# One-hot of an edge group: four 128x128 compares with a per-partition scalar in place of one 128x512 compare of two tensors

## What is computed

```python
h = jnp.einsum('ni,hio->hno', x, W)
e = attn_src[:, src_idx] + attn_dst[:, dst_idx]
e = jnp.where(e >= 0, e, NEG_SLOPE * e)
e = e * edge_weight[None, :]
e_exp = jnp.exp(e - jnp.max(e))
denom = jax.ops.segment_sum(e_exp.T, dst_idx, num_segments=num_nodes).T
alpha = e_exp / (denom[:, dst_idx] + 1e-10)
msg = h[:, src_idx] * alpha[..., None]
out = jax.vmap(lambda m: jax.ops.segment_sum(m, dst_idx, num_segments=num_nodes))(msg)
```

## Time and profile before

| | |
|---|---|
| runs, us | 868.2, 868.28, 870.37 (median 868.28) |
| span of the profiled execution, us | 864.6 |
| mean granted TensorE clock | 0.836 |
| busy: PE, DVE, POOL, ACT, us | 709.8, 596.9, 513.7, 231.3 |
| first and last start of a gather on POOL, us | 92.8, 641.7 |
| gathers (line 380), one-hots (line 992) | 392, 98 |

### The profile page before, as it was taken

One profiled execution on the slowest core, in us unless ns is written; L12 is line 12 of the kernel. 1 busy time (PEld: TensorE's weight loads), 2 busy tenths in 40 slices (PEclk: granted clock), 3 DMA queues, 4 the chain that ended last, 5 costly groups with the idle time before them and its releaser, 6 DMA issues.

```text
span 864.6 us, 18704 instructions
## 1 busy us (share of the span) xinstructions
PE 709.8 (82%) x4369; PEld 541.9 (63%) x4370; DVE 596.9 (69%) x1630; ACT 231.3 (27%) x915; POOL 513.7 (59%) x512
## 2 busy tenths in 40 slices
PE   3799687887878798868787878787876998999995
PEld 2576665555555565545565546465555987999994
DVE  7665277565657576657675757676667991999985
ACT  1133502111212122213132323232333442333331
POOL 5242537777777777778777777777751070333332
PEclk9899799776769776777787868787787998999998
DMA  6254325554556555554555545555420002000000
GB/s 202 69 170 80 95 59 132 128 123 121 123 125 129 125 124 129 121 124 119 122 128 128 128 115 126 126 119 120 115 79 1 1 1 78 19 31 26 32 25 21
DMA packets 104859, 82.97 MB, mean 96 GB/s; under 512 B 67133, under 2 KB 91566, under 8 KB 104561
## 3 DMA queue, kind: packets, MB, share of 16 engines
q0 software_dynamic: 18816, 52.21, 22.6%
q1 hardware_dynamic: 85873, 29.16, 15.6%
HBM read 74.47 MB, written 6.84 MB: 94 GB/s over the span
## 4 chain that ended last, share of the span: by engine, by line
POOL 37%; issue 26%; PE 21%; DVE 9%; DMA 4%; SPq 2%; POOLq 1%; DVEq 0%; ACT 0%; ACTq 0%
POOL G L380 37%; PE ps L561 8%; PE ps L574 7%; PE ps L414 2%; PE ps L420 2%; DVE wprod L1086 1%; DMA x<-in_x 1%; DVE G L1069 1%; DVE x L1073 1%; DVE stats L739 1%; DVE x L1027 1%; DMA dstm_d<-wide 1%; DMA htab<-hst 1%; DVE acc L1079 1%; DMA G<-htab,srcr 1%
## 5 line engine op out<-in xcount | busy, mean ns | idle before, releaser
L380 POOL DMA_INDIRECT G<-htab,srcr x392 | 419.3, 1070 | 149.9 <-issue 138.3
L480 PE MATMUL ps<-msg,oh 128*128 128x260 f32 x784 | 303.0, 525 | 74.0 <-DVE oh L992 73.7
L480 PEld LDWEIGHTS ps<-msg,oh 128*128 128x128 f32 x784 | 176.6, 249 | 105.0 <-issue 78.9
L930 DVE TENSOR_TENSOR msg<-G,msg 128x1024 f32<-128x1024 f32 x98 | 119.8, 1222 | 32.8 <-issue 22.2
L561 PEld LDWEIGHTS ps<-xnT,w 128*128 128x128 f32 x800 | 98.3, 201 | 3.8 <-issue 1.8
L561 PE MATMUL ps<-xnT,w 128*128 128x128 f32 x800 | 98.8, 285 | 2.1 <-ACT wide L721 1.6
L663 ACT ACTIVATE negR<-ps 128x1 f32<-128x1 f32 x98 | 16.8, 171 | 291.2 <-PE ps L476 253.9
L574 PE MATMUL ps<-w,wide 128*128 128x256 f32 x400 | 90.4, 379 | 1.0 <-DVE acc L1093 1.0
L393 POOL TENSOR_SCALAR G<-acc,mw 128x256 f32<-128x256 f32 x25 | 23.1, 926 | 99.6 <-DVE mw L1126 90.4
L449 PE MATMUL ps<-ad,ohT 128*128 x1464 | 74.7, 176 | 8.7 <-issue 4.5
L992 DVE TENSOR_TENSOR oh<-iota,dmr 128x512 f32<-128x512 f32 x98 | 67.4, 687 | 19.8 <-issue 19.0
(11 more groups left out here) (137 smaller groups left out, 801.8 us busy)
## 6 DMA issues: line engine op xcount, KB each, us to landing
dstb<-dstu_d SPq DMA_DIRECT2D x98, 128.0 KB
G<-htab,srcr POOLq DMA_INDIRECT x392
htab<-hst SPq DMA_DIRECT2D x25, 130.0 KB, 3.2
out<-G SPq DMA_DIRECT2D x24, 128.0 KB, 1.7
x<-in_x SPq DMA_DIRECT2D x4, 640.0 KB, 8.0
w<-in_L_ffn_w SPq DMA_DIRECT2D x4, 512.0 KB
kq<-w_d SPq DMA_DIRECT2D x1, 1600.0 KB, 6.3
dmr<-dstm_d SPq DMA_DIRECT2D x98, 2.0 KB
```

Source lines behind the costliest of these rows:

```text
L380: gp.indirect_dma_start(G[:, q % RING, k, :], None, htab, bass.IndirectOffsetOnAxis(ap=srcr[:, q, k:k + 1], axis=0)).then_inc(s_g[q % RING ...
L480: m = pe.matmul(ps[:, 3 + p, 0:ROW], oh[:, p, k, :], msg[:, p, k, :], start=(k == 0), stop=(k == TILES - 1))
L930: dve.tensor_tensor(msg[:, p, :, 0:HF].rearrange("p k (h o) -> p k h o", h=HEADS), G[:, q % RING, :, 0:HF].rearrange("p k (h o) -> p k h o ...
```

## The change

The list of destinations modulo 128 becomes float32 from the DRAM table on (`dstm_d`, `neg1`, `dmr`). The integer result `dm` is converted by one more VectorE instruction of 98x512 into `dmf`, which lies beside it in `wide`; `DLP`, the count that SP waits for, goes from 12 to 13. In the group loop, where one `tensor_tensor` compared a 128x512 view of `iota` with a broadcast of `dmr`, four `tensor_scalar` of 128x128 compare `iota` with one column of `dmr` each, as a scalar per partition. The semaphore `onehot_last` is raised by the fourth alone, and no wait stands between the four.

```diff
-    dstm_d = nc.dram_tensor("dstm_d", (NG * GE,), I32, kind="Internal").ap()
+    dstm_d = nc.dram_tensor("dstm_d", (NG * GE,), F32, kind="Internal").ap()
...
-        neg1 = sb("neg1", [1, PAD], I32)
+        neg1 = sb("neg1", [1, PAD])
...
-        dmr = sb("dmr", [P, LISTS, TILES], I32)
+        dmr = sb("dmr", [P, LISTS, TILES])
...
         dm = wide[0:NG, 0:GE].bitcast(I32)
+        dmf = wide[0:NG, GE:2 * GE]
...
-        DLP = 12
+        DLP = 13
...
-                sp.dma_start(dstm_d.rearrange("(g j) -> g j", j=GE), dm).then_inc(S["tables_stored"], 16)
+                sp.dma_start(dstm_d.rearrange("(g j) -> g j", j=GE), dmf).then_inc(S["tables_stored"], 16)
...
                     dve.tensor_tensor(mm[:, 1:2], mm[:, 2:3], dn[:, 5:6], ALU.subtract).then_inc(S["table_steps"], 1)
+                    dve.wait_ge(S["table_steps"], 12)
+                    dve.tensor_copy(dmf, dm).then_inc(S["table_steps"], 1)
...
-                    dve.tensor_tensor(oh[:, q % 2, :, :], iota[:, :].unsqueeze(1).to_broadcast([P, TILES, P]),
-                                      dmr[:, q, :].unsqueeze(2).to_broadcast([P, TILES, P]), ALU.is_equal).then_inc(S["onehot_last"], 1)
+                    for k in range(TILES):
+                        m = dve.tensor_scalar(oh[:, q % 2, k, :], iota[:, :], dmr[:, q, k:k + 1], None, ALU.is_equal)
+                    m.then_inc(S["onehot_last"], 1)
```

## The result

The changed kernel is slower: median 874.3 us of nine runs (870.55 to 878.77) against 868.2 us of nine runs of the kernel before (862.5 to 870.37). The ratio is 1.0096, with an interval of [1.0068, 1.0124], so about +8.3 us where the forecast had -5.0; the two medians themselves are 6.1 us apart. Four slow executions (one each of after_nodead, compares_i32_nodead, exp_flat_one and the kernel before) are left out of the times and ratios of this document. The profiled execution of after (span 877.0 us) is the longest of its nine, so its own difference of +12.4 us to the span of before is more than the typical one.

What follows compares the result with a forecast made beforehand. The prediction took POOL's issuing of gathers to bound the group loop. Its terms, -7.8 + 1.9 + 0.45 + 0.45 = -5.0 us, gave 863.3 us, with a range of 858.0 to 869.0.

Steps and rivals of the forecast that it cites:

- What bounds the kernel before, and who holds the gathers: Group loop: POOL's gathers set its length; VectorE's message product holds them up 36.8 us, the one-hot compare 7.8 us.
- What the change removes: Group loop: with the two-tensor one-hot compare go the 7.8 us that gathers lose behind it.
- What it puts there: Group loop: four scalar compares, lasting 0.92 us together, delay gathers by 1.9 us in all (0 to 3.7).
- The third: Group loop: slower; the four compares hold up the gathers' middle part, 9.5 us, giving 872.8 us; chance 0.10.
- the fourth rival: Group loop: slower; gathers cannot get in between the four compares, 16.3 us in place of 1.9, giving 877.7; chance 0.04.
- Cost in the loop: nothing: Group loop: one-hots 0.3 us longer, 29 us in all, fit into VectorE's 69.5 us of waits for rows.
- the ring of four groups: Group loop: the ring of messages keeps several groups of distance between VectorE and POOL, so a later VectorE costs nothing.
- The first rival: Group loop: VectorE falls differently; ten more gathers held by the message product add 5.3 us: 868.6, no change; chance 0.14.
- The tail: Behind the last gather: two longer one-hots on the path, 2 x 0.23 = 0.45 us (0.2 to 0.6).
- The front: Before the group loop: the added 98x512 conversion with its wait costs 0.45 us (0.4 to 0.5).
- Two bounds of the prediction: Group loop: upper bound 3.7 us for gathers held by the four compares; whole kernel: range's lower end 858.0 (861.4 - 3.2).

Runs made afterwards that it cites:

- after_nodead: The changed kernel without the never-taken branch in VectorE's program; 863.2 us, ratio 0.9970 to the kernel before.
- compares_i32_nodead: The kernel before with the four compares on the int32 list, no conversion, and without VectorE's never-taken branch; 865.0 us, ratio 0.9979.
- exp_flat_one: psum_both_flat with the one-hot's single compare reading the iota row from SBUF again; 837.9 us, ratio 0.9694 to the kernel before.
- The two PSUM kernels: psum_iota (859.2 us), and the same with the message product's exponentials also read from PSUM (831.4 us, ratio 0.9611).
- psum_iota: The kernel before with its single one-hot compare reading the iota row from a copy in PSUM; 859.2 us, ratio 0.9932.
- exp_flat_four: exp_flat_one with the four compares on the int32 list in place of the single compare; 827.3 us, ratio 0.9566 to the kernel before.
- compares_i32: The kernel before with only its one-hot changed into the four compares, list still int32, no conversion; 871.6 us, ratio 1.0086.
- before_dead3: The kernel before with three never-executed compares more per group in VectorE's never-taken branch; 871.3 us, ratio 1.0065.
- psum_iota_long_nodead: psum_iota without VectorE's never-taken branch and with the one-hot compare widened to last 0.2 us longer; 863.1 us, ratio 0.9983.
- the two pairs: psum_iota against itself with a one-hot 0.2 us longer (0.9932, 0.9995), and the same two without VectorE's never-taken branch (0.9927, 0.9983).
- front_only: The kernel before with float32 list and conversion but the single compare; 865.4 us, ratio 1.0010. Its second theory: first gather 1 to 2 us later.
- before_nodead: The kernel before without the never-taken branch in VectorE's program; 861.3 us, ratio 0.9966.
- psum_both_flat: psum_iota with the message product's exponentials also from PSUM, no never-taken branch, VectorE's loop written out; 824.0 us, ratio 0.9558 to the kernel before.

## Why the prediction was wrong, step by step

- **What bounds the kernel before, and who holds the gathers: right.** POOL's gathers set the loop, and they lose 47 us to VectorE instructions, 44.6 of them to the two that read two tensors from SBUF. The two PSUM kernels show it: -5.9 us for the one-hot, and 46 us of gather time for both. That POOL would go on setting it after the change was wrong for about half of the loop of the profiled after.
- **What the change removes: right in kind.** The 7.8 us behind the one-hot went to 0.3. It is real time where nothing else changes (psum_iota) or where the message product cannot take it back (exp_flat_four).
- **What it puts there: right, on the high side.** The four together last 0.93 us on average (91.0 us of 98 groups; 0.87 to 1.09), where I had 0.92, and about 1.0 with the delay by POOL; one takes 0.28 in the median, and 0.50 at the longest. They hold five gathers, 0.3 us, against my 1.9. The third and the fourth rival, both with the compares as a hindrance to POOL, fall with that: the median gather takes 946 ns beside the four.
- **"Cost in the loop: nothing": the step that failed, twice.** I priced the four compares by their time of execution, let the 69.5 us of waits take it up, and took the ring of four groups for enough distance between the one-hot and POOL. *First*, I did not price the instructions as code. Three more per group took the loop body over a step of code fetch, at some 2.3 us per turn: 0.9 us more ahead of the first message product and 1.3 ahead of the first one-hot. Worked out over nine turns that is 8.3 + 12 = 20 us, and 98 x 0.24 = 23.5 us of longer one-hots come on top: 44 us, against 42.3 us by which the waits of VectorE for rows shrank (69.5 to 27.2). This is a rough balance, as the stretch from the first gather to the last also grew, by 9.7 us. The slack was spent, unevenly; over about half of the loop the chain left POOL for the round of one-hot, maximum, exponentials and messages, and POOL stood for messages five times more. It took the code and the length together: of the chain from 92 to 650 us POOL's gathers have 57% before and 19% after, 27% in compares_i32, but 54% in before_dead3 and 52% in after_nodead. The sign that the prediction named, a second wait of POOL for messages, came true. Code that never runs costs 0.65% by itself; no rival of mine had this. *Second*, slack is not the only thing that 0.2 us on VectorE meet. Even with the slack largely there (64.6 us of waits in psum_iota_long_nodead), a one-hot longer by 0.2 us cost 2 to 6 us.
- **The first rival was the nearest to that second part.** It had the message product take the gain back through a VectorE that falls differently against the gathers, and in the profiled after the product holds 42.9 us, above the 42 that the prediction named as a sign of being wrong. Over the six kernels whose one-hot takes some 0.9 us, without a message product from PSUM, it holds 40.1 us on average (36.7 to 42.9); over the seven with 0.69 us, 36.9 us (32.7 to 40.3). The transposed one-hots and the sums have 4.5 us against 2.7. This is +5.0 us, the size of the gain, but single executions scatter by as much as the difference. That the length causes a loss is what the two pairs together show; that it goes through these meetings is argued, from these means and from exp_flat_four, where the meetings with the message product are away and the gain stays.
- **The tail was mis-sized.** I had 0.45 us for two longer one-hots. From the start of the last gather to that of the last one-hot it is 10.1 to 12.1 us in the six kernels with the longer one-hot, against 8.7 to 9.6 in the seven others, some 1.8 us in the mean. VectorE stands further behind when the gathers end; I counted only the instructions behind the last gather.
- **The front: probably mis-sized, too small.** Alone it is +0.1%, and its interval allows the 0.45 us as well as four times that. But the first gather starts at 94.8, 95.1 and 93.8 us in the three kernels with the conversion (after, front_only, after_nodead), 94.6 in the mean, and between 92.3 and 93.9, 92.9 in the mean, in the fifteen without: some 1.6 us, about what the second theory of front_only expected. Why it grows on the way from the conversion to the first gather is open.
- **The sum by what was measured.** One-hot freed -0.68%, length +0.63%, code +0.65%, front +0.10%: +0.70%, 6 us, against +0.96% [0.68, 1.24] measured. Each of the four has an interval of about 0.35% either way, the length, a difference of two ratios, a wider one, so the remaining 2 us are within what these runs leave open. Two bounds of the prediction were also off by little: 1.1 / 122 x 392 is 3.5 and not 3.7, and 861.4 - 3.2 is 858.2; neither changes its sum.

## What to carry to other kernels

Ahead of replacing one instruction by several in a hardware loop, count the loop body as code: look in the trace for idle time behind "issue" at the turn and at the packets of the instruction queue, and try the added length as code that never runs. Follow what waits for the replaced instruction through the other engines and back to its own, and do not count only how long its engine waits. An engine that holds another one up by meeting it can cost more when it gets slower, slack or not. Where VectorE and GpSimd meet at SBUF, the cheaper way out here was to move one operand to PSUM: no instruction more per group for the one-hot, no longer duration, and with the message product, at one ScalarE instruction more per group, 33 us instead of a loss.

## What the runs showed of the hardware

- At a turn of VectorE's loop of eight groups the engine stood 2.8 to 3.7 us ahead of its first big instruction (before), 2.8 to 3.5 with the shorter body of before_nodead, and at most 0.7 where the loop was written out (psum_both_flat); packets of code started in these gaps. Straight code of all 98 groups needed fewer packets (57) than the loop of ten turns (76, the same kernel with the loop).
- Instructions that are never executed cost 0.65%, about 5.6 us, when the body grew by 24, and nothing that shows (0.9998) when it grew by 8.
- A gather that, 0.13 us after its start, meets a VectorE operation with two tensors from SBUF ends 0.82 us after that operation's end; with one of the two in PSUM none was held by it (1.99 us at the longest in the earlier trace rows, 0.95 us in the middle of the same product).
- A 128x128 float32 compare with a scalar per partition takes 0.27 to 0.28 us, and four of them start some 0.2 us apart and last 0.87 to 0.95 us in most groups, with a gather passing through in 0.94 us. Where they met a gather it was the compare that took longer, up to 0.50 us.
